# A product of constants ahead of the scores in three small attentions of a four-layer decoder

## The reference

```python
scores = jnp.einsum('bhqd,bhkd->bhqk', q, k) * scale   # and the causal mask, where there is one
attn = jax.nn.softmax(scores, axis=-1)
out = jnp.einsum('bhqk,bkhd->bqhd', attn, v)
```

## Time and profile before

| | us |
|---|---|
| time, median of 3 runs | 2553.72 (2553.54 to 2557.07) |
| time of the profiled execution | 2549.37 |
| its span, first to last instruction | 2548.1 |
| differential attention of layer three, first score to last weighing | 1429.0 to 1686 |
| attention in layer three's feed-forward block | 2144.7 to 2208.3 |
| attention of layer four | 2377.1 to 2458 |
| mean granted TensorE clock over the span | 0.873 |

### The profile page before, as it was taken

The page is one execution under the profiler, slowest core; times in us unless marked ns, Lnnn a source line. Parts: engine busy times, 40 slices in busy tenths (PEclk is TensorE's granted clock), DMA queues, the critical chain, the costliest instruction groups (busy, mean ns, idle before and its releaser), DMA issues. The chain is left out here.

```text
span 2548.1 us, 35316 instructions
## 1 busy us (share of the span) xinstructions
PE 2059.2 (81%) x12705; PEld 1435.2 (56%) x12752; DVE 1544.0 (61%) x2880; ACT 1086.2 (43%) x2193; POOL 1074.3 (42%) x1101
## 2 busy tenths in 40 slices
PE   5666759999984999967546888878999988798777
PEld 2333346666763999943414454545777765555445
DVE  6877755554445777756785555544556555456546
ACT  3245626455432445535171354442444434432433
POOL 2766717556546767746543233321233222231000
PEclk8766679999986999978768888889999989989788
DMA  4222210000004565521001000020000000012000
GB/s 145 68 60 60 59 42 20 12 24 12 9 1 157 181 188 184 177 79 56 31 19 39 3 3 3 3 83 26 1 1 1 1 1 2 29 48 106 2 1 17
DMA packets 49868, 124.52 MB, mean 49 GB/s; under 512 B 5632, under 2 KB 18432, under 8 KB 47520
## 3 DMA queue, kind: packets, MB, share of 16 engines
q1 hardware_dynamic: 48160, 118.07, 14.5%
q0 software_dynamic: 1536, 4.20, 0.5%
HBM read 105.07 MB, written 16.12 MB: 48 GB/s over the span
## 5 line engine op out<-in xcount | busy, mean ns | idle before, releaser
L1837 POOL TENSOR_SCALAR l0f_probs<-l0f_probs,l0f_tot 128x128 f32<-128x128 f32 (+1 forms) x256 | 201.8, 807 | 141.7 <-DVE l0f_tot L1784 141.1
L3191 POOL TENSOR_TENSOR l2x_probs<-l2x_probs,l2x_rc 128x512 f32<-128x512 f32 x64 | 66.5, 1040 | 254.9 <-DVE l2x_rc L3092 254.9
L1306 DVE TENSOR_REDUCE l2a_a_max<-ps 128x6 f32<-128x768 f32 x128 | 119.5, 954 | 88.0 <-PE ps L1158 87.4
L1362 POOL TENSOR_SCALAR_AFFINE_SELECT l2a_a_probs<-l2a_a_probs 128x256 f32<-128x256 f32 (+1 forms) x192 | 88.3, 484 | 172.5 <-ACT l2a_a_probs L1268 148.7
L2054 PE MATMUL ps<-l0f_xh,l0f_wh 128*128 128x256 f32 x480 | 146.3, 305 | 0.1
L2171 POOL TENSOR_TENSOR l0f_wl<-l0f_raw,l0f_wh 128x1024 fp32r<-128x1024 f32 x60 | 142.0, 2386 | 0.0
L1708 ACT ACTIVATE l0f_probs<-ps,l0f_neg 128x128 f32<-128x128 f32 (+1 forms) x256 | 104.3, 424 | 87.1 <-DVE l0f_neg L1774 87.1
L2056 PE MATMUL ps<-l0f_xh,l0f_wl 128*128 128x256 f32 x480 | 136.5, 284 | 0.0
L2055 PE MATMUL ps<-l0f_xl,l0f_wh 128*128 128x256 f32 x480 | 136.5, 284 | 0.0
L3032 ACT ACTIVATE l2x_probs<-ps,l2x_neg,l2x_rs 128x256 f32<-128x256 f32 x128 | 71.0, 559 | 145.5 <-DVE l2x_neg L3082 145.4
L700 DVE TENSOR_TENSOR_SCAN l1x_h<-l1x_dA,l1x_dBu 128x512 f32<-128x512 f32 x64 | 116.6, 1860 | 8.6 <-issue 8.6
(11 more groups left out here) (722 smaller groups left out, 5828.0 us busy)
## 6 DMA issues: line engine op xcount, KB each, us to landing
l0f_raw<-in_e_l0f SPq DMA_DIRECT2D x60, 512.0 KB, 4.1
l0x_bc<-scratch_bc SPq DMA_DIRECT2D x32, 512.0 KB, 4.8
l0f_raw_d<-in_e_l0f SPq DMA_DIRECT2D x60, 256.0 KB, 3.0
scratch_rows<-zero SPq DMA_DIRECT2D x1, 3840.0 KB, 18.9
l0f_xb<-scratch_rows SPq DMA_DIRECT2D x15, 256.0 KB, 3.1
scratch_results<-l0f_yb SPq DMA_DIRECT2D x15, 256.0 KB, 2.3
l0f_slab<-in_g_l0f SPq DMA_DIRECT2D x8, 448.0 KB, 3.5
l2f_ew<-in_e_l2f SPq DMA_DIRECT2D x8, 384.0 KB, 3.0
```

What stands on the lines that cost most here:

```text
L1306: dve.tensor_reduce(M[:, 2 * half:2 * half + 2, j, :], src.rearrange("p a (c n) -> p a c n", c=NB_), AX.X, ALU.max).then_inc(*unit_max.tick())
L1362: last = pool.affine_select(part, part, [[0, m], [1, P]], ALU.is_ge, 0.0, base=0, channel_multiplier=-1)
L1837: last = pool.tensor_scalar(pr[:, u % 3, a, r], pr[:, u % 3, a, r], tot[:, u % 3, qt, a:a + 1], None, ALU.mult)
```

## The change

`Heads` gets a number `busy` (0 unless given), and the three calls named above pass 1. `score(n)` now issues that many products of constants into its own first bank, before its score products. It does so for every n; the wait for the exponential of n - 2 (from n = 2 on) comes first, and it now stands ahead of the wait for the maxima instead of behind it. The lead-in keeps its three products. In the attention of layer one `busy` is 0, and only the order of the two waits changes.

```diff
-    def __init__(self, H, KV, hd, causal, batches, values):
+    def __init__(self, H, KV, hd, causal, batches, values, busy=0):
+        self.busy = busy
...
             def score(n):
                 b, x = n // NC, n % NC
                 z, (m, half), (kt, p) = b % 3, hs.octets[x // SPO], hs.parts[x % SPO]
+                if n >= 2:
+                    pe.wait_ge(*weighed(n - 1))
+                k.warm(ps[:, 4 + 2 * (n % 2), :], hs.busy)
                 if x == 0:
                     pe.wait_ge(*rows(2 * PAR * (b + 1)))
-                if n >= 2:
-                    pe.wait_ge(*weighed(n - 1))
...
-        small_attention(k, "l2a_a_", Heads(32, 8, 8, True, 2 * NB, lambda b, kt: 2 * (b % NB) + kt), qq, kk, vv, oo)
+        small_attention(k, "l2a_a_", Heads(32, 8, 8, True, 2 * NB, lambda b, kt: 2 * (b % NB) + kt, 1), qq, kk, vv, oo)
...
-            small_attention(k, "l2f_a_", Heads(16, 16, 16, True, NB, lambda b, kt: 2 * b + kt), qk[:, 0], qk[:, 1], vv, o)
+            small_attention(k, "l2f_a_", Heads(16, 16, 16, True, NB, lambda b, kt: 2 * b + kt, 1), qk[:, 0], qk[:, 1], vv, o)
...
-        small_attention(k, "l3a_a_", Heads(16, 1, 16, False, NB, lambda b, kt: 2 * b + kt), q, kk, vv, o)
+        small_attention(k, "l3a_a_", Heads(16, 1, 16, False, NB, lambda b, kt: 2 * b + kt, 1), q, kk, vv, o)
```

## The result

The changed kernel took **2566.12 us** (median of 6 runs, 2562.05 to 2568.4) against 2554.35 for the kernel before beside it (6 runs, 2550.83 to 2557.07): ratio **1.0044**, 95% interval 1.0033 to 1.0055. It is 11 to 12 us slower. The forecast was 2558 with 2541 to 2575, and slower had the largest chance. The profiled execution took 2566.79 us.

The account below looks back on a forecast made before the run. TensorE sets the pace, slowed by 130 us at half clock. Products cost +27.8 us, recovered clock gives -24.2, the entry adds 0.7: +4.3 on the median 2553.7, so 2558 us, range 2541 to 2575.

Parts of the forecast that it names:

- No cost of the swapped waits: Ahead of each score: swapping the waits for exponential and maxima costs nothing, since both were needed before the same score.
- The price of a product: On TensorE ahead of each score: 0.22 us at full clock, 0.40 behind a layer-four unit; 35 us in all.
- The exposed share: Part of the products' time that lengthens each stage: 0.8 differential, 0.6 second attention, 0.55 layer four.
- the 1.1 that its clock was to give back: Layer three's second attention: half of its 6.4 us at half clock goes, giving back 1.1 us.
- Layer four: Its attention: products cost +5.6 us; a third of long half-clock stretches and all four short ones go, -10.5 us.
- the half clock removed in the differential attention: Entry and two of three batch-end falls stay, short mid-batch ones go: 36 us less at half, -12.6 us.
- what was to show it: Changed profile: clock means near 0.92 differential, 0.85 layer four; half clock at entry and most batch ends; full-clock batches about 34 us.
- What half clock costs: All three attentions: 0.35 us of time for each us at half clock, 0.48 in short stretches holding a weighing.
- the 47 us that could be given back: All three attentions: the most the change can give back if all half clock goes, 27 + 2.2 + 18.
- products don't lift it once it is down: From layer one's lead-in, 13.6 us at 0.50 with TensorE busy 13.27: products can only prevent a fall.
- A better clock: Rival: falls at batch ends and the entry go too, three quarters of 47 us back: -9, 2545 us; chance 0.24.
- No answer of the clock at all: Rival: products ahead of each score are pure load on TensorE's queue: +32, 2585 us; chance 0.09.

Follow-up runs that it names:

- experiment 1: Changed kernel with busy 0 in all three calls, so only the order of the two waits differs from the kernel before: 2553.02 us, ratio 0.9991.
- Experiment 6: Kernel before with three products at each score of the differential attention, none in the other two stages, one run: 2591.83 us.
- experiment 4: Changed kernel with the product kept only in layer four's attention: 2547.35 us, ratio 0.9979 against the kernel before.
- experiment 2: Changed kernel with the product kept only in the differential attention: 2564.63 us, ratio 1.0037 against the kernel before.
- experiment 8: Kernel before plus, in the differential attention, eight entry products and four at each of two batch-end waits, plus layer four's products: 2543.32 us, ratio 0.9967.
- experiment 10: As experiment 8 but without layer four's products: 2545.11 us, ratio 0.9978 against the kernel before.
- experiment 12: Repeat of experiment 8, the same kernel: 2541.93 us, ratio 0.9974 against the kernel before.
- experiment 7: As experiment 8 but without the four products at the second batch-end wait (s = 2): 2551.9 us, ratio 1.0006 against the kernel before.
- experiment 11: As experiment 8 but without the four products at the first batch-end wait (s = 0): 2546.21 us, ratio 0.9991 against the kernel before.

## Why the prediction was right, and where it was not

The total came out in the range (2566 against 2541 to 2575) and on the likeliest side, 8 us above the number. Which stages lose and which gains was right. The largest stage was 6 us off, which the wide range holds. By its steps:

- *No cost of the swapped waits*: right (experiment 1).
- *The price of a product, 0.22 us of TensorE's stream and 0.40 behind a unit*: right at those places. Where a step of the differential attention holds nothing but TensorE's work it grew by 0.21 to 0.22 us. Behind a weighing it was more: from a weighing's start to the score 1.44 us before and 1.76 after. That 0.32 was taken to be 0.22.
- *The exposed share*: near. The differential attention grew by 13.4 us with 6.8 us less at half; at 0.35 that gave back 2.4, so the products cost 15.8, and 19 was forecast. The steps are not alike in it: of the twelve of a batch near the end that ran at full clock (1622.34 to 1654.21, 31.87 us, and 30.17 before) four grew by nothing, six by 0.10 to 0.22, and the two with a weighing by 0.31 and 0.33. In sum that is 1.70, 0.64 of twelve times 0.22. It is a little more in truth, since that batch's first step still had 0.6 us at half before: its first two steps took 4.98 us, and 4.80 in the batch before it, which began at full clock. That makes it 1.88, or 0.71. Experiment 6 gives 0.18 a product, 0.8 of the price. The second attention paid 3.2 us, as forecast for its products; the 1.1 that its clock was to give back didn't come (6.8 us at half, before and after), so it is 3.2 longer and not 2.
- *Layer four*: right in mechanism, and near in size. 25 us of half clock were to go (a third of the long stretches and all short ones), 23.6 went. A stretch of 13.6 still stands near its start. Forecast -4.9 in sum, measured -3.2 in the profile and -6.0 in the medians of experiment 4, whose interval holds both. The stage took 80.8 to 81.0 us in each of six profiles without the product and 74.3 to 77.6 in each of the seven with one of full height.
- **The step that failed is the half clock removed in the differential attention.** I let two falls of three at batch ends and the entry stay, 36 us go and 12.6 us come back. (The sum isn't what these words say: it takes a third off the entry too, two thirds of 61.5. With the entry whole, 48 us stay, 29 go and 10 come back.) In the profiles 6.8 us went (13.7 in experiment 2) and 2.4 to 4.8 us came back. All falls at batch ends stayed. Where the timeline was read, one product stands ahead of TensorE's wait for VectorE with its score, the next behind it, and none in it. That place and number both count is what the experiments show: 96 products at the scores took 7 to 14 us of half clock away, 288 took 44, and 56 at the entry and in the waits took 34 in two profiles and 14 in a third. That one term is 8 to 10 us too good; products that cost 3 us less than forecast make up for a part. Of what was to show it, half clock left at the entry and at batch ends was right, but the mean of 0.92 was wrong (0.87), 0.85 in layer four right, and of whole batches at full clock of about 34 us there was none.
- *What half clock costs, and three readings of the rows.* The 0.35 us for each us at half came from two batches that differ in mid-batch. At a batch's end it costs less: a batch with none took 33.1 us (experiments 8, 10 and 12, with eight products in its waits), one of before with 7.6 took 34.90, so 0.24 for each, and the 47 us that could be given back were an overestimate. The 77 us at half are 75.1 in the clock's record. The clock fell 1.8 us after the first score (at 1430.8), not 0.6. And "products don't lift it once it is down" was read from a stretch inside a longer one. In the same lead-in of layer one the clock rose at 126.9, in the midst of six products:

```profile
123.50:126.90 3.40, 3.34 (x12) 1.01 (x9) 3.37 (x6) 0.69 (x1) 2.77 (x3) 0.50 0.00 1
126.90:130.30 3.40, 1.28 (x8) 0.51 (x6) 2.64 (x3) 1.32 (x3) 3.40 (x4) 0.99 0.72 162
```

- *The rivals.* A better clock (2545) fell. No answer of the clock at all (2585) fell as a rule for the whole kernel, but it is nearly what happened in its largest stage. The Trainium skill, "TensorE: Matmul & The Clock Gate", section "HAM oscillation — how this bites in real kernels", blames idle gaps between bursts; its example has gaps of 3 to 5 us. That agrees with the batch ends in kind, though the waits there are 1.6 to 1.7 us long. It agrees with how the entry begins as well: the fall comes behind the wait of 1.47 us for the maxima, and with that wait filled (experiments 7, 8 and 10 to 12) it comes some 7 us later, counted from the first score. It doesn't explain how long the entry lasts: the clock stayed at 0.50 for 23.8 us with TensorE busy 22.91.

## What to carry to other kernels

Work that only keeps TensorE's clock up pays where the engine would wait anyway, or has idle time to spare (19% in layer four): look for the waits that stand ahead of each fall and put the load in them, before it lengthens the steps that are limited by TensorE. Price it per stage, because the same line gained 3 to 6 us in one attention here and lost 11 to 13 in another; a switch per stage is worth its one argument. One profile isn't enough to count half-clock time: the same kernel had 61 and 41 us of it.

## What was not expected of the hardware

- The narrow product (128 rows, 32 columns of weights) held the clock in layer four as well as the full one (one profile), and took about the same time (median 389 ns, and 379).
- Products at one of two neighbouring waits only moved the fall to the next step (64.9 us at half with the first place, 75.1 with the second; 41.0, 41.0 and 61.4 in three profiles with both).
- One kernel's differential attention differed by 20 us of half clock and 7 us of time between two executions (experiments 8 and 12). Whether a change in one stage shifts the falls in later ones can't be told from that.
- In the entry of the differential attention eight more products ahead of the first score (1.89 us) moved the fall from 1430.8 to 1436.8 and halved it, from 20.5 us to 10.2. They did not prevent it: behind them the clock fell out of a stretch in which TensorE was busy 2.74 of 3.40 us.
